# A graph network, linear attention and LSTM kernel: first stage in a pipeline, scores from the dense product, weights in halves, a 16-wide state

## The reference, cut to what matters

```
h_raw = ln(x) @ W.T + b
h     = h_raw / |h_raw| * sigmoid(ln(x) @ mag_w.T + mag_b) * 1.5
score = h[src] @ a_s + h[dst] @ a_t          # softmax over the edges of one dst
agg   = segment_sum(h[src] * softmax(score), dst)
g     = clip(expmap0(h + agg))               # graph part

y = ln(x); for i in range(4):                # attention part
    y = y + linear_attention(ln(y), Wq, Wk, Wv, Wo)
    y = y + gelu(ln(y) @ W1 + b1) @ W2 + b2

x = x + g + y
out = x + weights(lstm(ln(x)))               # an LSTM over all 6250 rows in order, 256 units,
                                             # its states weighted by running counts
```

## Time and profile before

| | us |
|---|---|
| median of 3 runs | 16385.18 (16385.08 to 16394.63) |
| profiled execution, its time | 16384.31 |
| profiled execution, its span | 16382.4 |

### The profile page before, as it was taken

The page is one execution under the profiler, slowest core; times in us unless marked ns, Lnnn a source line. Parts: engine busy times, 40 slices in busy tenths (PEclk is TensorE's granted clock), DMA queues, the critical chain, the costliest instruction groups (busy, mean ns, idle before and its releaser), DMA issues. The chain is left out here.

```text
span 16382.4 us, 1975327 instructions
## 1 busy us (share of the span) xinstructions
PE 13391.4 (82%) x904808; PEld 11671.6 (71%) x904808; DVE 7184.2 (44%) x46836; ACT 6996.2 (43%) x42403; POOL 2774.1 (17%) x4549
## 2 busy tenths in 40 slices
PE   2258667586651599999999999999999999999998
PEld 1147556475540588888888888888888888888887
DVE  3365565655643433333333333333333333333335
ACT  0136344363541044444444444444444444444443
POOL 2147264472641000000000000000000000000000
PEclk9988888798875799999999999999999999999999
DMA  1124243342431200000000000000000000000000
GB/s 23 48 83 150 62 131 111 91 150 62 133 99 25 77 2 2 2 2 2 2 2 2 2 2 2 2 2 2 2 2 2 2 2 2 2 2 2 2 2 17
DMA packets 677248, 541.82 MB, mean 33 GB/s; under 512 B 541596, under 2 KB 593184, under 8 KB 664870
## 3 DMA queue, kind: packets, MB, share of 16 engines
q1 hardware_dynamic: 450870, 316.75, 6.6%
q0 software_dynamic: 221600, 223.50, 5.6%
q10 hardware_dynamic: 4650, 0.12, 0.0%
HBM read 285.95 MB, written 252.14 MB: 33 GB/s over the span
## 5 line engine op out<-in xcount | busy, mean ns | idle before, releaser
L1373 PE MATMUL p_g<-ring,wh 128*32 128x32 f32 x800000 | 8373.3, 198 | 452.2 <-DVE ring L1472 190.3
L1373 PEld LDWEIGHTS p_g<-ring,wh 128*32 128x32 f32 x800000 | 7678.2, 109 | 1360.5 <-DVE ring L1472 1050.6
L1414 ACT ACTIVATE cell<-p_g 128x3 f32<-128x3 f32 x12500 | 2173.1, 174 | 5644.7 <-PE p_g L1373 5644.7
L1466 DVE CUSTOM_DVE_ANT_1 cj<-cell 128x4 f32<-128x4 f32 x12500 | 2038.5, 163 | 5746.2 <-ACT cell L1414 5746.2
L1417 ACT ACTIVATE tc<-cell 128x1 f32<-128x1 f32 x12500 | 2482.1, 199 | 0.0
L1472 DVE SCALAR_TENSOR_TENSOR ring<-og,tc 128x1 f32<-128x1 f32 x12500 | 1999.0, 160 | 777.7 <-ACT og L1419 2.3
L1507 POOL COPY hist<-ring 128x6 f32 x2501 | 471.6, 189 | 10529.9 <-POOLq L1506 10529.9
L355 POOL DMA_INDIRECT eb<-node_tab,eidx x1650 | 2064.1, 1251 | 626.7 <-issue 445.6
L1419 ACT ACTIVATE og<-p_g 128x1 f32<-128x1 f32 x12500 | 2047.1, 170 | 4.2 <-PE p_g L1373 4.0
L1347 PE MATMUL p_g<-xq,idn 128*32 128x48 f32 (+3 forms) x80032 | 1850.1, 205 | 35.4 <-PEq L1360 15.6
L1347 PEld LDWEIGHTS p_g<-xq,idn 128*32 128x32 f32 x80032 | 1354.7, 109 | 240.6 <-issue 17.9
(11 more groups left out here) (213 smaller groups left out, 7696.3 us busy)
## 6 DMA issues: line engine op xcount, KB each, us to landing
edge_tab<-eb SPq DMA_DIRECT2D x96, 1391.1 KB
edge_tab<-eb SPq DMA_DIRECT2D x96, 758.8 KB
eb<-node_tab,eidx POOLq DMA_INDIRECT x1650, 5.5
xp_tab<-xo SPq DMA_DIRECT2D x50, 500.0 KB, 2.6
xq<-xp_tab SPq DMA_DIRECT2D x1251, 8.0 KB, 1.7
xq<-xp_tab SPq DMA_DIRECT2D x1250, 12.0 KB, 1.7
x<-w_in SPq DMA_DIRECT2D x8, 1024.0 KB
node_tab<-hrow SPq DMA_DIRECT2D x50, 126.0 KB
```

Of the source, the lines that this page charges most:

```text
L1373: m = pe.matmul(to[32 * q:32 * q + 32], wh[:, k, D * q + 32 * c:D * q + 32 * c + 32], ring[:, (s - 1) % TS, k:k + 1].broadcast_to([128, w] ...
L1414: act.activation(cell[:, s, k, 0:6:2], gate_at(h, u, k)[:, :, 0], ACT.Tanh).then_inc(l_s[k], 1)
L1466: dve.tensor_tensor_reduce(cj[:, k, :].rearrange("p (a b) -> p a b", a=2), cell[:, s, k, 0:4].rearrange("p (a b) -> p a b", a=2), cell[:, ...
```

## The change

Four parts; computed is the same.

1. First stage. All loops over tiles are written out. x, dst and the stored rows go as two DMAs each, rows 0 to 111 and 112 to 124. dst is loaded whole and VectorE picks every fiftieth entry. z is gone: `normed(t + 3)` normalises y in place, `measured(t + 2)` and `gathered(t + 1)` are the statistics of the result, and TensorE transposes tile t + 1 ahead of the product of tile t. `located()` (the second comparison) stands in the loop at tile 18. The two score vectors are multiplied into the weights once (wg has 259 columns), so that each row's scores come out of the product, and are scaled later for all rows at once. Rows are scaled two of five by ScalarE, three by VectorE, and stored five tiles at a time.
2. Weights: the attention's are issued at the start of pass c of the layer before (the first ahead of the AHEAD stores), the feed-forward's at the start of pass a; SP waits for each at the end of that pass.
3. The barrier: one semaphore an engine (two in turn) that counts three arrivals, for one semaphore a pair.
4. The scan: W = 16, so that `gate` streams 16 columns and `place_x` 4 a gate; `fill` stays at 96.

```diff
+        RB = 112
+        by_rows = (slice(0, RB), slice(RB, R))
@@ first stage, SP
+                    for rows in by_rows:
+                        sp.dma_start(y[rows], x.rearrange("(i p) c -> p i c", p=R)[rows]).then_inc(s_x, 16)
...
+                    for g in range(NT // HG_):
+                        sp.wait_ge(g_rowa, g + 1)
+                        sp.wait_ge(g_row, g + 1)
+                        for rows in by_rows:
+                            sp.dma_start(node_tab[g * HG_ * R:(g + 1) * HG_ * R, :].rearrange("(j p) c -> p j c", p=R)[rows],
+                                         hrow[rows, g % 2]).then_inc(g_st[g % 2], 16)
@@ first stage, TensorE
+                    turned(0)
+                    for t in range(NT):
+                        if t + 1 < NT:
+                            turned(t + 1)
+                        dense(t)
@@ first stage, ScalarE
+                    for rows in by_rows:
+                        act.dma_start(dsti[rows], dst_pj[rows]).then_inc(g_sub, 16)
...
+                    turned(0)
+                    turned(1)
+                    for t in range(NT):
+                        if t + 2 < NT:
+                            turned(t + 2)
+                        act.wait_ge(g_h, t + 1)
+                        act.activation(junk[:, t % 2, :], x1[:, t, :], ACT.Square, accum_out=ss[:, t:t + 1])
+                        act.activation(sc[:, t, :], ph[t % 2][0:R, D:D + 3], ACT.Copy).then_inc(g_hf, 1)
...
+                    for g in range(NT // HG_):
+                        if g >= 2:
+                            act.wait_ge(g_st[g % 2], 32 * (g // 2))
+                        for j in range(ACT_ROWS):
+                            t = g * HG_ + j
+                            a = act.activation(hrow[:, g % 2, j, 0:D], x1[:, t, :], ACT.Copy, scale=cf[:, t:t + 1])
+                        a.then_inc(g_rowa, 1)
@@ first stage, VectorE
+                    for t in range(NT + 1):
+                        if t < NT:
+                            dve.bn_stats(bst[:, t % 4, :], y[:, t, :]).then_inc(s_dve, 1)
+                        if t > 0:
+                            dve.wait_ge(s_dve, t)
+                            a = dve.bn_aggr(mv[:, t - 1, :], bst[:, (t - 1) % 4, :])
...
+                    for k in range(KC):
+                        for h in range(2):
+                            dve.tensor_tensor_reduce(junk2[:, 2 * k + h, :], wg[:, k, 0:D], asb[:, h, :], 1.0, 0.0, ALU.mult, ALU.add,
+                                                     wg[:, k, D + 1 + h:D + 2 + h])
...
+                    for t in range(NT):
+                        if t + 3 < NT:
+                            normed(t + 3)
+                        if t + 2 < NT:
+                            measured(t + 2)
+                        if t + 1 < NT:
+                            gathered(t + 1)
+                        if t == LOCATE:
+                            located()
+                        dve.wait_ge(g_ph, t + 1)
+                        dve.tensor_tensor(x1[:, t, :], ph[t % 2][0:R, 0:D], gb[:], ALU.add).then_inc(g_h, 1)
@@ second stage, the barrier
+                    n = passed[name] % 2
+                    passed[name] += 1
                     others = [o for o in ENG if o != name]
                     for o in others:
-                        eng.sem_inc(bar[name, o], 1)
-                    for o in others:
-                        eng.wait_ge(bar[o, name], 1)
-                        eng.sem_inc(bar[o, name], -1)
+                        eng.sem_inc(arrived[o][n], 1)
+                    eng.wait_ge(arrived[name][n], len(others))
+                    eng.sem_inc(arrived[name][n], -len(others))
@@ second stage, SP
+                    first = begin(attention_loads(0) + [(blk[:], diag)])
                     for place in AHEAD:
                         edge_store(sp, place)
-                    with sp.Fori(0, DEPTH) as layer:
...
+                    landed(first)
+                    for layer in range(DEPTH):
                         barrier("sp", sp)
+                        coming = begin(forward_loads(layer))
                         barrier("sp", sp)
                         units(sp, layer, 0, lambda place: edge_store(sp, place))
+                        landed(coming)
                         barrier("sp", sp)
+                        coming = begin(attention_loads(layer + 1)) if layer + 1 < DEPTH else 0
                         units(sp, layer, 1, lambda place: edge_store(sp, place))
+                        if coming:
+                            landed(coming)
                         barrier("sp", sp)
@@ the scan
-                W = 32
+                W = 16
```

More of the change, by code:

```diff
@@ new lines, in dense @@
+                    def dense(t):
+                        pe.wait_ge(n_zt, t + 1)
+                        if t >= 2:
+                            pe.wait_ge(g_hf, t - 1)
+                        for k in range(KC):
+                            m = pe.matmul(ph[t % 2][0:R, 0:D + 3], zt[:, t % 2, k, :], wg[:, k, :], start=(k == 0), stop=(k == KC - 1))
+                        m.then_inc(g_ph, 1)
+                    turned(0)
[3 more added lines that the diff above has]
+                        dense(t)
@@ L221, in _ @@
                 @block.scalar
                 def _(act):
+                    for rows in by_rows:
+                        act.dma_start(dsti[rows], dst_pj[rows]).then_inc(g_sub, 16)
                     act.dma_start(nid[:], node_id).then_inc(g_ids, 16)
-                    with nc.allow_non_contiguous_dma(reason="the last edge of each stretch of 50"):
-                        act.dma_start(subd[:], dst_pj.rearrange("p (a b) -> p a b", b=SC)[:, :, SC - 1]).then_inc(g_sub, 16)
-                    act.wait_ge(g_sub, 16)
+                    act.wait_ge(g_tab, 1)
@@ new lines, in _ @@
+                    for q in (n_z, n_pt, n_zt, s_dve):
+                        dve.sem_inc(q, -NT)
+                    dve.wait_ge(g_sig, 1)
+                    then(dve.tensor_scalar(nrm[:], nrm[:], 1e-12, None, ALU.max))
+                    then(dve.reciprocal(cf[:], nrm[:]))
+                    dve.scalar_tensor_tensor(cf[:], mg[:], 1.5, cf[:], ALU.mult, ALU.mult).then_inc(g_cf, 1)
+                    dve.wait_ge(g_cf, 1)
+                    for h in range(2):
+                        a = dve.scalar_tensor_tensor(scn[:, :, h], sc[:, :, 1 + h], ba[:, h:h + 1], cf[:], ALU.add, ALU.mult)
@@ L338, in gps_kernel @@
                 ecar = sb(ctx, "ecar", [R, D])
-                e_in, e_init = sem("e_in"), sem("e_init")
+                e_init = sem("e_init")
                 e_got = [sem(f"e_got{s}") for s in range(NSLOT)]
@@ new lines, in begin, with landed @@
+                    def begin(pairs):
+                        with nc.allow_non_contiguous_dma(reason="a layer's vectors by partition"):
+                            for to, frm in pairs:
+                                sp.dma_start(to, frm).then_inc(m_w, 16)
+                        return 16 * len(pairs)
+                    def landed(count):
+                        sp.wait_ge(m_w, count)
+                        sp.sem_inc(m_w, -count)
+                    first = begin(attention_loads(0) + [(blk[:], diag)])
```

220 lines of the change are left out of this document (99 added, 121 removed).

## The result

The changed kernel takes 15,816.95 us (median of 4 runs, 15,808.75 to 15,822.99) against 16,389.9 us before (4 runs): ratio 0.965, 95% interval 0.9637 to 0.9663. Forecast were 15,530 us; rival 1, whose only difference is a gain of 13 ns instead of 60 ns a step of the scan, gave 15,830. The time lies outside the forecast's own range (15,330 to 15,700).

A forecast was written before the change was run, and what follows sets the result against it. The prediction took the recurrent scan, 64% of the span, as the main part, with 1.11 us of TensorE a step on its path; 16,384 - 380 (first stage) - 95 (weights) - 375 (scan) gave 15,530 us, range 15,330 to 15,700.

The forecast's parts named there:

- rival 1: Scan: 16 columns gain only the tail, 13 ns a step or 80 us, giving 15,830; chance 0.24.
- the 60 ns a step: Scan: gain from 16 columns for 32, taken from bounds of 0 and 90 ns; 6250 steps make minus 375 us.
- the tail: Scan: the placing matmul's duration shrinks with its width, about 13 ns a step.
- some of the pace of the 104 matmuls that stand before the second gates: Scan: less contention of weights and columns, 8.0 for 8.8 ns a matmul, guessed at most 80 ns a step.
- Rival 2: Scan: 16 columns bring TensorE to half clock, 2.18 us a step, plus 3,080 us, giving 18,990; chance 0.30.
- For it: Argument for half clock in the scan: the clock falls where TensorE works in part (busy 108 of 200, clock 0.76).
- Against: Argument against half clock in the scan: what the profile calls busy stays, with no pause over 0.4 us in a step.
- The index: First stage: first search's index written at 50 us instead of 77.9, through faster loads; bounds 35 and 78.
- which nothing undercuts: First stage: index, two chains of 50 GpSimd gathers (76 us each) and the location between them, 213 us in all.
- the tiles at 1.7 us: First stage: pitch from tile to tile 1.7 us instead of 6.4, bounds 1.4 to 2.7.
- a store at 4.2 us: First stage: ten stores of five tiles, 42 us after 192, ending at 234; bounds 37 to 60 us in all.
- Rival 3: Layers and first stage: SP's loads hold up edge stores, first stage at its bad end, 15,674; within the forecast's 0.45.

The follow-up runs named there:

- e4: The changed kernel with a state of 48 columns instead of 16; 17,430.94 us, ratio 1.0624 to the kernel before.
- e1: The kernel before with the 16-column state alone (32 columns until then); 16,309.87 us, ratio 0.9944.
- e9: The changed kernel with a state of 12 columns instead of 16; 15,800.45 us, ratio 0.9639 to the kernel before.
- e2: The changed kernel with a state of 8 columns instead of 16; 18,891.32 us, ratio 1.1516 to the kernel before.
- e3: The changed kernel with a state of 4 columns instead of 16; 18,847.96 us, ratio 1.1491 to the kernel before.
- e6: The changed kernel with x, dst and the stores as one DMA each, not split at row 112; 15,836.69 us, ratio 0.9664 to the kernel before.
- e7: The changed kernel with the second search at tile 45 instead of 18; 15,826.34 us, ratio 0.9653 to the kernel before.
- e8: The changed kernel with the small search tables loaded ahead of x and the second search at tile 36 instead of 18; 15,821.11 us, ratio 0.9654 to the kernel before.
- e13: The changed kernel with 12 columns, small tables ahead of x and the second search at tile 24; 15,787.61 us, ratio 0.9632 to the kernel before.
- e5: The kernel before with the layers' weights loaded in halves alone; 16,299.01 us, ratio 0.9943.

## Why the prediction was right in sign and wrong in size, by its own steps

**The scan, where it failed.** The direction, the clock and the reading of the pace were right; the step that failed is the 60 ns a step: some 13 for the tail and 47 for "some of the pace of the 104 matmuls that stand before the second gates", a guess of 8.0 for 8.8 ns out of bounds of 0 to 90 (by the code it is 96 records, not 104). Both together measured 13. Start to start four weight loads take

| columns | granted clock | four loads, ns | step, us | kernel |
|---|---|---|---|---|
| 48 | 1.00 | 44.4 | 1.933 | e4 |
| 32 | 1.00 | 33.3 | 1.688 | before |
| 16 | 1.00 | 33.3 | 1.675 | after, e1 |
| 12 | 1.00 | 33.3 | 1.671 | e9 |
| 8 | 0.50 | 53.3 | 2.166 | e2 |
| 4 | 0.50 | 53.3 | 2.160 | e3 |

in the even part of a step (after its 96th record), so that halving 32 columns wins nothing there. The rows had said so: 16 placing matmuls of 16 columns at 9.3 ns from one to the next beside 8.8 ns at 32. I had written "a narrower matmul isn't issued faster" and then took 47 ns for contention that no row showed, because a range of 0 to 90 has its middle there. Of the whole miss of 287 us, 292 are this term (375 less 83); the others miss by 19 one way and 11 the other. Rival 1's 13 ns came out as 13, but by luck in part, for they are not the tail that it was made of. By the starts (e1) they are all pace, gained between the 33rd and about the 73rd record of a step; the stretch from the last start before the second gates to these gates, which holds the tail, stays (251 and 252 ns). At half clock it is the other way round: from 8 to 4 columns the starts stay (1268 and 1267 ns) and that stretch falls from 268 to 262. Why 16 columns are faster in that part of the step at full clock is open.

The Trainium skill (TensorEngine Tiling (Array Packing), "Instruction Overhead") has a matmul of one column cost as much as one of 60. Between 12 and 32 columns the traces agree (33.3 ns for four). Between 32 and 48 they don't: 33.3 becomes 44.4. Following it, and taking rival 1, would have given 15,830.

**The clock.** Rival 2 did not happen with 16 columns and did with 8. The 0.30 that I gave it was not too much: the mechanism and the price (2.18 us a step forecast, 2.166 measured at 8) are real, one halving further on. Its "For it" was sound and its "Against" (what counts as busy stays as it is) was no reason: e2 is busier than the changed kernel and is held at half. The prediction also says that the clock moves in the trace of before under full-width matmuls only. It had a row against that: 0.50 in the scan's first microseconds, under the narrow ones, and 1.00 later.

**First stage, 399 for 380.** The index was forecast for 50 us and came at 49.98, in part by luck. The forecast put its lateness down to loads that crawl and worked the 50 us out from their rate with the split; e6, without the split, has it 6 us earlier still. What made it late was the read that picks every fiftieth entry, some 45 us long, which reading dst whole replaces. The chain "which nothing undercuts", 213 us, is what ended last: last gathers in at 215.06. I had the stores end later, at 234. They end at 208, for two terms were too long: the tiles at 1.7 us, measured 1.04 to 1.44, on average 1.20 (140 to 174 us, TensorE busy 33.57 of 34 at clock 1.00), under the 1.3 to 1.4 that were counted for VectorE alone, and a store at 4.2 us, measured 2.9. The store goes back to reading row 10:20 and not asking why only 0.36 of the DMA engines were busy. The Trainium skill (DMA: Bandwidth & Descriptors, "Why a DMA increments its semaphore by 16 and not by 1") says that a transfer uses the largest number of engines up to 16 that divides the slowest dimension of both its sides: 5 for 125 rows, 16 for 112. The traces agree, 0.31 of the engines busy with 125 rows (e6) and 1.01 with 112 and 13. I had bounded with 173 GB/s from weight loads onto 128 partitions, where 210 was there to be had. e7 and e8 show that the chain is the bound from both sides: VectorE's wait taken away brings nothing, the index alone made early brings nothing while its middle link is late, and both together (e13) bring 13.7 us.

**Weights in halves, 84 for 95.** Of 96.9 us of idle time ahead of the four layers 4.9 stay: 92 gone, 95 counted. 8 came back: passes b are 5.1 us longer in sum (1306.1 to 1311.2, from their first maximum on), the first three passes c 6.1 (1370.7 to 1376.8), the others 3.5 shorter. So the cost that I put at 0, at most 60, is about 8. Rival 3's 20 us a layer did not come. e5 shows the same 85 us without the other edits.

**The barrier** was counted at nothing; it was not taken alone. e5, with the old barrier, takes 4675.6 us for the second stage and the changed kernel 4676.4, so nothing of it shows.

## What to carry to other kernels

Where the only evidence for a gain is that its bounds are wide, take the end that the nearest row stands at, not the middle: here the row said "same pace", and the rival that believed it came within 0.1% of the time. Before narrowing a matmul, ask what holds the pace (one wider run, as e4, and one narrower, as e2, tell it) and look at the granted clock each time, since a narrower stream can cost 19% of the kernel (e2) while the busy share rises. A forecast number that comes true isn't yet its mechanism: the index came at the forecast time for another reason. And an engine's longest wait is not the bound: follow the chain that it waits for, and move all of its links together.

## What the runs showed of the hardware that I had not expected

- The same instruction stream gets 2.4 GHz with 12, 16, 32 and 48 columns a matmul and stays at 1.2 GHz with 8 and 4, over 13.5 ms, while the profile has TensorE busy for 991 of 1000 us. What the chip looks at is left open.
- At half clock four narrow pairs take 53.3 ns with 8 and with 4 columns, and one pair of 128 weight columns takes 213 ns with 16: four times as long for the same weights. It would fit a price for the weight columns of a pair, with the four column groups working side by side; no run separates the two. At full clock that price would be 26.7 ns for four, and 33.3 were measured, so there something else holds; pairs with 16 weight columns would tell, and weren't tried.
- Ten stores of 125 rows moved at 106 GB/s with 0.38 of the engines busy; the same stores as 112 and 13 rows at 202 GB/s with 0.75.
- A DMA that picked 4125 single integers (16 KB) out of dst took some 45 us beside the load of x; the whole of dst (806 KB) landed within 11 us beside the same load (kernel before and e6).
